# Thirty-two columns of the array per matmul in the pair stage, in place of sixty-four

## The reference

```python
latent_kv = x @ w_kv_down
kv = latent_kv @ w_kv_up
k, v = (kv[..., :HD], kv[..., HD:])
q = (x @ w_q).reshape(Bx, Tx, N_HEAD, HEAD_SIZE)
att = jnp.einsum('bqhd,bkhd->bhqk', q, k) * scale
att = jnp.where(causal, att, -jnp.inf)
att = jax.nn.softmax(att, axis=-1)
y = jnp.einsum('bhqk,bkhd->bqhd', att, v)
```

## Time and profile before

| | before |
|---|---|
| median of the runs | 1698.41 us |
| the profiled execution | 1699.01 us |
| its span | 1697.8 us |
| PE busy, share | 1654.4 us, 97% |
| DVE / POOL / ACT busy | 1225.1 / 867.1 / 846.5 us |
| line 670 (scores), matmuls | 3072 |
| line 692 (values), matmuls | 4608 |
| lines 714, 718, 724 (jobs), matmuls | 512, 256, 1024 |
| granted TensorE clock, mean | 0.997 |

### The profile page before, as it was taken

How to read it: one execution, slowest core, us unless ns; L and a number is a source line. 1 busy time by engine, 2 the same in 40 slices (tenths; PEclk the granted TensorE clock), 3 DMA queues, 4 the chain that set the end, 5 groups by cost and what they waited for, 6 DMA issues and landing times.

```text
span 1697.8 us, 44169 instructions
## 1 busy us (share of the span) xinstructions
PE 1654.4 (97%) x18099; PEld 1111.3 (65%) x18099; DVE 1225.1 (72%) x2674; ACT 846.5 (50%) x1872; POOL 867.1 (51%) x1127
## 2 busy tenths in 40 slices
PE   9999999999999999999999999999999999999997
PEld 5566685768556667566846567666784656766667
DVE  5899947727699985763779997675468999577445
ACT  5677624233577753422457774432246767443232
POOL 3788852142188884232238888324114888731420
PEclk9999999999999999999999999999999999999999
DMA  6566571231565654041356665305044666620504
GB/s 194 125 157 156 140 200 70 39 62 53 157 157 142 146 143 164 1 75 25 91 139 160 151 148 137 136 2 100 0 138 126 146 149 151 156 96 2 100 1 126
DMA packets 143881, 189.31 MB, mean 112 GB/s; under 512 B 34528, under 2 KB 107712, under 8 KB 142656
## 3 DMA queue, kind: packets, MB, share of 16 engines
q1 hardware_dynamic: 125472, 179.14, 42.6%
q10 hardware_dynamic: 18208, 7.35, 1.7%
HBM read 88.32 MB, written 13.16 MB: 60 GB/s over the span
## 4 chain that ended last, share of the span: by engine, by line
PE 81%; DVE 9%; ACT 5%; POOL 2%; issue 2%; DMA 1%; SPq 1%; ACTq 0%; POOLq 0%; DVEq 0%
PE scores L470 13%; PE scores L670 12%; PE bank L692 12%; PE bank L470 5%; PE bank L714 4%; PE bank L724 3%; PE bank L718 3%; ACT prob L921 2%; DVE prob L805 2%; PE scores L441 2%; PE scores L1792 2%; PE scores L1732 2%; PE scores L1371 1%; PE bank L1732 1%; PE scores L1856 1%
## 5 line engine op out<-in xcount | busy, mean ns | idle before, releaser
L869 POOL COPY placed<-prob 32x768 f32<-32x768 f32 x448 | 367.9, 821 | 205.3 <-DVE prob L805 171.0
L301 POOL TENSOR_TENSOR rstd<-rstd,minus_half 128x2 f32<-128x2 f32 (+1 forms) x100 | 71.8, 720 | 487.3 <-DVE rstd L300 485.2
L692 PEld LDWEIGHTS bank<-placed,v_t 128*64 128x64 f32 x4608 | 256.7, 138 | 41.7 <-issue 41.5
L692 PE MATMUL bank<-placed,v_t 128*64 128x128 f32 x4608 | 270.9, 274 | 4.4 <-ACT tmp L951 2.8
L670 PE MATMUL scores<-k_t,q_t 64*64 64x512 f32 (+3 forms) x3072 | 269.9, 489 | 2.0 <-DVE neg_max L798 2.0
L805 DVE STREAM_TRANSPOSE prob<-prob 128x1536 f32<-128x1536 f32 x128 | 220.0, 1757 | 36.3 <-ACT prob L921 36.3
L798 DVE CUSTOM_DVE_ANT_0 mod_rows<-scores,hx 128x128 f32<-128x128 f32 (+7 forms) x256 | 190.6, 744 | 35.2 <-PE scores L670 34.9
L869 POOL COPY placed<-hx 32x768 f32<-32x768 f32 x224 | 184.0, 822 | 29.6 <-DVE hx L805 13.0
L921 ACT ACTIVATE prob<-mod_rows,neg_max 128x128 f32<-128x128 f32 (+2 forms) x192 | 137.3, 715 | 111.1 <-DVE neg_max L798 111.1
L798 DVE CUSTOM_DVE_ANT_0 x<-scores,hx 128x128 f32<-128x128 f32 (+7 forms) x256 | 192.6, 752 | 0.0
L670 PEld LDWEIGHTS scores<-k_t,q_t 64*64 64x64 f32 x3072 | 103.0, 133 | 134.1 <-issue 124.1
(11 more groups left out here) (253 smaller groups left out, 3077.9 us busy)
## 6 DMA issues: line engine op xcount, KB each, us to landing
placed<-prob SPq DMA_DIRECT2D x576, 96.0 KB, 2.5
f<-in_L_ffn_f SPq DMA_DIRECT2D x16, 2048.0 KB, 13.7
placed<-hx SPq DMA_DIRECT2D x288, 96.0 KB, 2.2
inverse_wide<-inverse_scratch SPq DMA_DIRECT2D x64, 256.0 KB, 4.1
slots_scratch<-high_rows SPq DMA_DIRECT2D x16, 512.0 KB, 6.8
inter<-slots_scratch SPq DMA_DIRECT2D x32, 256.0 KB, 4.7
mod_rows<-mod_scratch SPq DMA_DIRECT2D x32, 128.0 KB, 5.0
out<-x SPq DMA_DIRECT2D x16, 256.0 KB, 2.1
```

Source lines behind the costliest of these rows:

```text
L301: step = pool.do(lambda e, ts=ts: nc.gpsimd.tensor_tensor(rstd[:, ts], rstd[:, ts], minus_half[:, ts], op=ALU.pow), var, filled)
L692: last = nc.tensor.matmul(out_bank[rows_, at_:at_ + P], v_t[pair % 2][:, j, rows_], placed[m % 2][:, :, head, first_block(m, i) + j, :], s ...
L869: nc.gpsimd.tensor_copy(placed[m % 2][target * GROUP:(target + 1) * GROUP, source, :, :, :], prob[m % 3][source * GROUP:(source + 1) * GRO ...
```

## The change

A tuple of four slices of 32 (`QUARTERS`) takes the place of the two halves of 64 wherever a slice chooses columns of the array: the sides of the scores, the column tiles of the values (each head's 64 columns of v become two of 32, and the head is `k // 2`), and the sides of the three kinds of jobs. The rows of the score products stay 64 per head. Each matmul moves the same columns past as before, and the number of matmuls doubles. No semaphore, bank or other engine's instruction is changed; the lines behind the new one move down by one.

```diff
--- before.py
+++ after.py
@@ -545,6 +545,7 @@
         SCORE_BANKS = 3
         Q_SCALE = -(HD0 ** -0.5)
         ROWS_OF = (slice(0, HD0), slice(HD0, P))
+        QUARTERS = tuple(slice(k * P // 4, (k + 1) * P // 4) for k in range(4))
         MOVED = ("moved_even", "moved_odd")
         ACROSS = [(src, dst) for dst in range(GROUPS) for src in range(GROUPS) if src != dst]
         MOVES, COPIES = ACROSS[:-3], [(g, g) for g in range(GROUPS)] + ACROSS[-3:]
@@ -666,7 +667,7 @@
                 ends = {piece[1] // 512: piece[1] for piece in pieces}
                 for tile, at_, lo, hi in pieces:
                     for head, rows_ in enumerate(ROWS_OF):
-                        for side in ROWS_OF:
+                        for side in QUARTERS:
                             last = nc.tensor.matmul(score_tiles[head][side, at_ // 512, at_ % 512:at_ % 512 + hi - lo],
                                                     q_t[buf][rows_, tile * P + side.start:tile * P + side.stop],
                                                     k_t[buf][rows_, lo:hi], start=True, stop=True)
@@ -688,9 +689,9 @@
                 for i, tile in enumerate(tiles_in(m)):
                     at_ = out_slot(m, tile) * P
                     for j in range(tile + 1):
-                        for head, rows_ in enumerate(ROWS_OF):
+                        for k, rows_ in enumerate(QUARTERS):
                             last = nc.tensor.matmul(out_bank[rows_, at_:at_ + P], v_t[pair % 2][:, j, rows_],
-                                                    placed[m % 2][:, :, head, first_block(m, i) + j, :],
+                                                    placed[m % 2][:, :, k // 2, first_block(m, i) + j, :],
                                                     start=j == 0, stop=j == tile)
                 last.then_inc(flow["values_done"], 1)
 
```

## The result

The change is slower: 1704.08 us median of 9 runs (1699.96 to 1706.25) against 1698.6 (1696.03 to 1699.67), a ratio of 1.0033 with a 95% interval of 1.0025 to 1.0042. That is 5.5 us more where 3.2 less were forecast. The profiled execution has a span of 1702.8 us, 5.0 above's.

What follows compares the result with a forecast made beforehand. PE, busy 97% of the span and 81% of the chain, was taken as the bound. Terms 0 + 0 - 1.2 - 2.0 = -3.2 us took the median 1698.41 to 1695.2, range 1690 to 1710.

Steps and rivals of the forecast that it cites:

- rival B: Score pieces of 128 columns: PE can't be handed matmuls faster than 27 ns each; 14.0 us more, 1709.2; chance 0.17.
- A wave costs what its columns cost, not its number of matmuls: Pair stages: matmuls in different tiles run beside each other, so values, q, k and v keep their steady time: 0 us.
- Ends and beginnings of groups: Tiling switches to or from scores, 192 times: shorter first weight loads gain 5.2 us, later tails cost 4.0; net -1.2 us.
- Switches that go: Ahead of batches 2 to 4, first jobs alternating with line 1914 no longer switch tiling: 2.2 us gained, taken as -2.0.
- PE does not stop in between, so it counts: Ahead of batches 2 to 4: the 2.2 us from switches shortens the whole; at worst line 1914 waits instead, 0.
- Score products: Scores as 8 tiles of 64 rows by 32 columns: eight starts take 49 ns, under the shortest wave's 109; 0 us.
- What lies beside: Beside PE's stream: later score-bank semaphores for DVE are hidden, and 1.2 MB more instructions in 802 us cost 0 us.
- a change of DVE's or POOL's timing by some ns is covered by PE: Pair stages: the end moves only by what PE's own stream gains or loses.
- Rival C: Whole stream: matmuls sustained at only 30 ns each, so values and v fall behind too; about 1742; chance 0.04.
- D: Group switches: shorter load counts whole and wave tails are hidden; -5.2 - 2.2 = -7.4, 1691.0; chance 0.12.

Runs made afterwards that it cites:

- scores: Only the score products at 32 columns, against the kernel before: 1701.05 us, ratio 1.0009.
- short pieces: The kernel before with every score piece cut into pieces of 128 keys, no tile of 32 columns: 1704.44 us, ratio 1.0034.
- values and jobs: Values and jobs at 32 columns, score products left at 64, against the kernel before: 1701.14 us, ratio 1.0008.
- the first jobs alone: Only the jobs of pair 0 (first q, k and v of a batch) at 32 columns, against the kernel before: 1698.73 us, ratio 0.9993.
- the jobs alone: All jobs at 32 columns, values and scores at 64, against the kernel before: 1716.01 us in one run, +16.4.

## Why the prediction was wrong, point by point

1704.1 us was measured, 8.9 above the forecast of 1695.2. That it lies inside the stated 1690 to 1710 is luck: the range reached so far because of rival B, whose mechanism cost 2.5 us and not 14.0.

- **A wave costs what its columns cost, not its number of matmuls: right**, also for eight tiles of 64 by 32, the shape no row had shown (2.75 us for 80 matmuls, 2.74 for 48).
- **"Ends and beginnings of groups", -1.2 us: right in sign, about -2.3 measured.** The uncovered load shrank by 26 ns (27 forecast), but only on the way from scores to jobs (96 times, start to start); the way back did not gain it. The later tail costs 14 ns after q and k (64 times), and after v the group is 22 ns shorter (32 times; why is open).
- **"Switches that go", -2.0 us: right for its stretch and wrong for the end.** The stretch gives 2.2 us. "PE does not stop in between, so it counts" was false: some 13 us later PE waits for k's copy, 5.2 us in place of 3.0, because DVE waits for a store that an instruction packet holds up. I had looked for such a wait at line 1914 alone. The edit by itself gives 0.9 us, within its interval of nothing.
- **Score products, 0 us: mis-sized.** It measures +2.5 us: 77 ns in the third round of each pair. Rival B named the place and the reason, at 219 ns a piece. In the trace half of the products behind the short piece start 17 ns apart instead of 7. Read as a limit that is 17 ns a product, and not the 27 ns a matmul that I took from the fastest row. The first round's short piece costs next to nothing; that its products, and those of the next, are at hand when the array has emptied is argued, not tested.
- **"What lies beside", the instruction queue, 0 us: this is the step that failed.** I foresaw the 1.2 MB more (1.22 came, 217 packets in place of 143) and priced them as bandwidth, 1.5 GB/s. Their price is latency: 110 of SP's 123 long issues, which last 1.36 us on average in place of 0.59, have a packet of 16 KB beside them, and a store with such a packet beside it lands 1.1 to 1.9 us late. The waits for moved blocks grew by 7.4 us.
- **The other part of that step was also false:** "a change of DVE's or POOL's timing by some ns is covered by PE", and with it every delay off PE. I read PE's small waits for DVE as slack. They showed that the chain DVE, ACT, SP, PE of a round was just in time: 0.56 us more of SP's time a round, by one more transfer of 16 KB, costs 2.9 us.
- **The sum, from the two traces:** in the stages 7.4 (waits for moved blocks) + 2.2 (for k's copy) - 1.1 (for DVE's minima, 0.9 us in place of 2.0) + 2.5 (scores) - 2.3 (ends and beginnings) = 8.7 us of the 9.3 measured. Ahead of them -2.2 us. The rest of the program, whose instructions are the same, took 2.1 us less in this execution (it varies by some 4 us from trace to trace), which makes the 5.0 of the spans; the medians say 5.5.
- Rival C's price (30 ns a matmul throughout) did not occur, nor D.

What is shown: the fetches come with longer issues with or without narrow tiles, and longer issues cost time without fetches. With 143, 167, 191, 193 and 217 fetches (before, scores, short pieces, values and jobs, change) the waits for moves are 1.3, 3.5, 5.4, 6.5 and 8.7 us. One trace each says little of the small ones: the first jobs alone and the jobs alone have 2.6 and 3.1 us with 145 and 157 fetches. The store of x is the nearest to a direct test, within the same code: one part in 16 of the transfer lands late in all 16 stores that have a packet beside them from the first 1.6 us on, and in none of the 29 others. What is argued only: that the moves are held up in the same way, that the packet is also what lengthens SP's issue (they coincide in 110 of 123 cases), and how, inside the DMA engines. No 16 KB packet was put beside the moves by itself.

## What to carry to other kernels

Cutting matmuls into narrower tiles of the array gained nothing here, where the tiles already filled it: the time of a wave stays, and only its instructions multiply. Instructions are DMA traffic in large packets, and must be priced by whom they delay: look for a queue that issues transfers back to back just ahead of when they are needed. An engine that is busy for 97% is no proof of slack in the chain that feeds it, and what it gains in one place counts only if its next waits don't grow: follow it to the first wait behind. Neighbouring groups should have the same rows and columns of the array, since each change of either cost 0.10 to 0.15 us.

## What the runs showed of the hardware

- Eight tiles of 64 rows by 32 columns run beside each other at full pace (a wave of eight with 512 columns begins 429 ns after the one before).
- Behind a piece of 128 keys in eight tiles, four of the eight products of the next wave start 17 ns apart, where they start 7 ns apart elsewhere; it cost 77 ns a round.
- A store of 256 KB lands in 2.1 us, and in 3.2 to 4.0 us where an instruction packet starts 0.6 to 1.6 us after its issue; 15 of its 16 parts land on time.
- A copy of 16 KB from DRAM to DRAM goes as 1 KB packets and disturbs the moves little; one of 64 bytes goes as 4-byte packets and made the kernel 0.5% slower at 96 copies.
- In the kernel after the issue of a move of 96 KB takes 0.59 us, and up to 2.19 us while an instruction packet is in transit.
